# MoE 0's experts: each tile's first weights brought by a transfer instead of a VectorE copy, and VectorE's order within a tile changed

## What is computed

```
logits = tokens @ router_w.T;  probs = softmax(logits)
rw, re = top_k(probs, 2);      rw = rw / rw.sum()
out = tokens
for e in range(8):
    h = gelu(tokens @ w1[e] + b1[e])         # w1[e] is 256 x 256 in layer 0, 256 x 1024 in layer 1
    y = h @ w2[e] + b2[e]
    out = out + combine[:, e:e+1] * y        # combine holds rw for the two chosen experts, else 0
```

## Time and profile before

| | us |
|---|---|
| median of 3 runs | 2578.47 |
| lowest and highest | 2574.83, 2580.76 |
| the profiled execution | 2575.45 |
| its span in the profile | 2573.7 |

### The profile page before, as it was taken

How to read it: one execution, slowest core, us unless ns; L and a number is a source line. 1 busy time by engine, 2 the same in 40 slices (tenths; PEclk the granted TensorE clock), 3 DMA queues, 4 the chain that set the end, 5 groups by cost and what they waited for, 6 DMA issues and landing times. The chain is left out here.

```text
span 2573.7 us, 84276 instructions
## 1 busy us (share of the span) xinstructions
PE 2011.3 (78%) x28546; PEld 1511.0 (59%) x28547; DVE 2174.8 (85%) x3745; ACT 1674.1 (65%) x2530; POOL 789.6 (31%) x587
## 2 busy tenths in 40 slices
PE   4739999999999999999966158703598309999994
PEld 3316666666666666666645146501286209999993
DVE  4989999999999999999977747678798757777775
ACT  5439999999999999999965335403255535555551
POOL 2652212113222232422221734405111642222220
PEclk8869999999999999999987579955799559999996
DMA  2002323323323223223222434330000561111115
GB/s 78 0 19 77 89 69 87 87 70 87 83 74 87 77 79 89 72 83 89 70 79 81 146 107 116 109 139 3 0 0 26 171 217 49 51 48 47 49 46 202
DMA packets 284540, 202.95 MB, mean 79 GB/s; under 512 B 153632, under 2 KB 260208, under 8 KB 284208
## 3 DMA queue, kind: packets, MB, share of 16 engines
q1 hardware_dynamic: 271216, 164.16, 22.4%
q0 software_dynamic: 12960, 35.73, 3.7%
q10 hardware_dynamic: 288, 2.10, 0.2%
HBM read 69.05 MB, written 108.60 MB: 69 GB/s over the span
## 5 line engine op out<-in xcount | busy, mean ns | idle before, releaser
L583 DVE TENSOR_TENSOR plow<-prob 128x1024 f16<-128x1024 f32 (+1 forms) x1024 | 1127.2, 1172 | 3.7 <-ACT prob L494 3.7
L494 ACT ACTIVATE prob<-scores 128x1024 f32<-128x1024 f32 x1024 | 999.9, 1025 | 88.5 <-PE scores L626 58.4
L646 PEld LDWEIGHTS outp<-vs,prob 128*128 128x128 bf16 x7680 | 515.1, 98 | 280.2 <-issue 220.8
L646 PE MATMUL outp<-vs,prob 128*128 (+1 forms) x7680 | 603.6, 193 | 24.9 <-DVE plow L583 12.2
L626 PE MATMUL scores<-qT,kT 128*128 (+1 forms) x2048 | 610.7, 380 | 7.5 <-DMA kT<-shift_rows 2.7
L648 PE MATMUL outp<-vs,plow 128*128 (+1 forms) x7680 | 601.2, 193 | 0.0
L648 PEld LDWEIGHTS outp<-vs,plow 128*128 128x128 f16 x7680 | 502.8, 97 | 57.5
L439 POOL TENSOR_TENSOR osum<-osb 128x128 f32<-128x128 f32 x64 | 250.4, 3912 | 811.5 <-DVE rec L588 811.5
L1495 POOL DMA_INDIRECT expert_rows<-m1eyo,m1edest x71 | 107.6, 1516 | 315.4 <-DVE m1eyo L1467 285.4
L1366 PE MATMUL m1eph<-m1exT,m1ew1c 128*128 128x128 f16 x3408 | 203.0, 220 | 0.4 <-ACT m1exT L1403 0.4
L1366 PEld LDWEIGHTS m1eph<-m1exT,m1ew1c 128*128 128x128 f16 x3408 | 194.1, 98 | 1.1 <-ACT m1exT L1403 0.6
(11 more groups left out here) (375 smaller groups left out, 3325.9 us busy)
## 6 DMA issues: line engine op xcount, KB each, us to landing
sorted_rows<-zero SPq DMA_DIRECT2D x128, 522.0 KB, 4.7
m1dstg<-in_L_ffn_W_dram SPq DMA_DIRECT2D x32, 512.0 KB
staged<-qk SPq DMA_DIRECT2D x73, 128.0 KB, 2.4
m0exr<-sorted_rows SPq DMA_DIRECT2D x71, 130.5 KB
m1exr<-sorted_rows SPq DMA_DIRECT2D x71, 130.5 KB, 2.1
m0cgot<-expert_rows SPq DMA_DIRECT2D x8, 1024.0 KB, 5.6
m1cgot<-expert_rows SPq DMA_DIRECT2D x8, 1024.0 KB, 7.9
tok<-in_x_dram SPq DMA_DIRECT2D x4, 1024.0 KB, 9.5
```

Of the source, the lines that this page charges most:

```text
L494: act.activation(prob[g % PBUF][:, :], scores[g % 2][:, :], ACT.Exp, scale=1.0 / (QK_SCALE * QK_SCALE)).then_inc(prob_ready, 1)
L583: dve.tensor_tensor(l[:, 0:n], p[:, 0:n], high(p)[:, 0:n], ALU.subtract).then_inc(low_ready, 1)
L646: pe.matmul(to, high(prob[g % PBUF])[:, cols], v, start=(g == 0 and i == 0 and j == 0), stop=False, skip_group_check=True)
```

## The change

In MoE 0 (`narrow`, F // 128 < 4) a DMA started by SP, `fetch`, brings each tile's first weights from the weights in SBUF to one of four places `w1c`, three tiles ahead, right behind the tile's row load. It waits on `h_ready` for the place to be free, loads the expert's number into a register of SP, and moves 2 KB in each of 128 partitions. TensorE's `first` waits for the transfer's semaphore `w1_in`. VectorE's copy, its wait on `h_ready` and its increment of `w1_ready` are gone from `aim` in MoE 0, and `aim(i+2)` stands at the end of VectorE's step instead of its head. `aim` loads the expert into one of four registers, and `rows_out`, in both MoEs, uses the register that `aim` loaded two tiles before instead of loading its own. MoE 1 keeps its copy and its order.

```diff
+    narrow = NF < 4
+    NX = NY = NR if narrow else 2
-        w1c = [sb(f"w1c{u}", [P, 2, KB, F], F16) for u in range(2)]
+        NW = NX
+        w1c = [sb(f"w1c{u}", [P, 2, KB, F], F16) for u in range(NW)]
@@ SP
+            def fetch(i, u):
+
+                if not isinstance(i, int) or i >= NW:
+                    sp.wait_ge(h_ready, (i - NW + 1) * NQ)
+                    sp.sem_inc(fetching, 1)
+                e = expert_of(sp, w_reg, i)
+                sp.dma_start(w1c[u % NW][:, :, :, :], w1[:, ds(e, 1)].squeeze(1)).then_inc(w1_in[u % NW], 16)
+
             def step(i, u, it, left):
                 if left > NX - 2:
                     load(i + NX - 1, u + NX - 1)
+                    if narrow:
+                        fetch(i + NX - 1, u + NX - 1)
 
             for i in range(NX - 1):
                 load(i, i)
+                if narrow:
+                    fetch(i, i)
@@ TensorE
-            def first(i, u):
+            def first(i, u, it):
                 pe.wait_ge(xt_ready, i + 3)
-                pe.wait_ge(w1_ready, i + 1)
+                if narrow:
+                    pe.wait_ge(w1_in[u % NW], uses(it, u, NW) * 16 + 16)
+                else:
+                    pe.wait_ge(w1_ready, i + 1)
@@ VectorE
-            reg = dve.alloc_register(name + "dve_expert")
-            y_reg = dve.alloc_register(name + "dve_y_expert")
+            regs = [dve.alloc_register(name + f"dve_expert{u}") for u in range(4)]
 
             def aim(i, u, it):
-                e = expert_of(dve, reg, i)
-                if not isinstance(i, int) or i >= 2:
-                    dve.wait_ge(h_ready, i * NQ - NQ)
-                dve.tensor_copy(w1c[u % 2][:, :, :, :], w1[:, ds(e, 1)].squeeze(1)).then_inc(w1_ready, 1)
+                e = expert_of(dve, regs[u % 4], i)
+                if not narrow:
+                    if not isinstance(i, int) or i >= 2:
+                        dve.wait_ge(h_ready, i * NQ - NQ)
+                    dve.tensor_copy(w1c[u % 2][:, :, :, :], w1[:, ds(e, 1)].squeeze(1)).then_inc(w1_ready, 1)
                 dve.wait_ge(x_in[u % NX], uses(it, u, NX) * 16 + 16)
@@ rows_out
-                e = expert_of(dve, y_reg, i)
+                e = the_expert(dve, regs[u % 4])
@@ VectorE's step
-                if left > 1:
+                if left > 1 and not narrow:
                     aim(i + 2, u + 2, it)
                 if left > 0:
                     halve(i + 1, u + 1)
                 rows_out(i, u, it)
+                if left > 1 and narrow:
+                    aim(i + 2, u + 2, it)
```

More of the change, by code:

```diff
@@ L1268, in experts @@
     NQ = NF // 2
-    NX = NY = NR if NF < 4 else 2
+    narrow = NF < 4
+    NX = NY = NR if narrow else 2
     U = 2 * NR
@@ L1295, in experts @@
         w1_ready = sem("w1_ready")
+        w1_in = [sem(f"w1_in{u}") for u in range(NW)]
+        fetching = sem("fetching")
         h_ready = sem("h_ready")
@@ L1334, in load @@
                 sp.dma_start(xr[u % NX][:, :], sorted_dram[ds(row, P), :]).then_inc(x_in[u % NX], 16)
+            w_reg = sp.alloc_register(name + "sp_expert")
+            def fetch(i, u):
[4 more added lines that the diff above has]
+                sp.dma_start(w1c[u % NW][:, :, :, :], w1[:, ds(e, 1)].squeeze(1)).then_inc(w1_in[u % NW], 16)
             def step(i, u, it, left):
@@ L1366, in first @@
                                 last = pe.matmul(ph[(u * NQ + j) % 4][:, h * ET:(h + 1) * ET],
-                                                 w1c[u % 2][:, w, k, f * P:(f + 1) * P], xT[u % 2][:, x, :],
+                                                 w1c[u % NW][:, w, k, f * P:(f + 1) * P], xT[u % 2][:, x, :],
                                                  start=(k6 == 0), stop=(k6 == 3 * KB - 1))
@@ L1389, in step @@
                 if left > 0:
-                    first(i + 1, u + 1)
+                    first(i + 1, u + 1, it)
                 second(i, u)
@@ L1395, in _ @@
             turn(1, 1, 0)
-            first(0, 0)
+            first(0, 0, 0)
             pipelined(pe, step)
```

## The result

| | us |
|---|---|
| after, median of 4 runs (lowest, highest) | 2602.22 (2599.34, 2605.92) |
| before, on the same chip, median of 4 | 2577.06 (2574.83, 2580.76) |
| ratio, 95% interval | 1.0094 [1.0075, 1.0113] |
| the profiled execution of after (span) | 2604.65 (2602.9) |

The account below looks back on a forecast made before the run. The prediction took VectorE and its register loads in MoE 0 to set the pace; looped tiles 7.8, written-out tiles 2.9 and start 0.7 gave +11.4 us, hence 2590 us, range 2575 to 2608.

Parts of the forecast that it names:

- The ring: In MoE 0, `dest`, gelu, cast, low half and next `b1c` follow in series: 2.37 us a tile looped, 2.28 written out.
- `dest` to cast: In MoE 0's tile: `dest` 0.21, handover to ScalarE 0.17, two gelus 0.63, their end to VectorE's cast 0.10 us.
- rival 2: ScalarE's two further waits cost nothing and the loop's branch vanishes in the wait: 2.05 to 2.12 a tile, 2569 us; chance 0.08.
- Low half to `b1c`: On VectorE, waits and issue of L1467, then register load, wait and issue of `b1c`: 0.86 us looped, 0.77 written out.
- rival 1: VectorE's register load runs ahead of L1467's execution: 2.22 us a looped tile, about 2579 us, no change; chance 0.17.
- Cast to low half: On VectorE in MoE 0, from the start of the cast to the low half: 0.33 us a tile.
- The loop's sum: MoE 0's looped tiles average 2.40 us against 2.26 before, 7.8 us over 56 tiles.
- the branch: The loop's branch back every eighth tile: its own idle hidden in VectorE's wait for the gelu, 0.03 us a tile staying.
- Written-out tiles: MoE 0's tiles outside the loop: 12 at the steady pace go from 2.04 to 2.28 us, 2.9 us together.
- Start: At the start of MoE 0, three fetches go out with the first rows: 0 to 2 us, taken as 0.7.
- The transfer at nothing: In MoE 0's loop, the 256 KB fetch a tile costs nothing: DMA total 1.65 to 2.08 us fits into 2.40.
- rival 3: SP's fetch issue takes 1.2 us instead of 0.95 and the branch costs SP too: step 2.5 to 2.6, 2596 us; chance 0.05.

Follow-up runs that it names:

- no fast cast: The changed kernel with MoE 0's cast and bias copy written as two-input operations with the same result; 2.67 us a looped tile.
- scatter later: The changed kernel with GpSimd starting a tile's MoE 0 scatter only once the cast of the tile two on is done; ratio 1.0077 to before.
- aim first: The changed kernel with `aim(i+2)` put back at the head of VectorE's step in MoE 0; 2585.92 us, ratio 1.0027 to before.

## Why the prediction was right in sign and low in size

- **What bounded the kernel before: right.** VectorE with its register loads. Taking one load away gave 0.39 a tile, more than its visible gap of 0.2: 0.31 of it ahead of L1467 (0.65 to 0.34), 0.08 behind it.
- **The ring: right.** The forecast had the ring at 2.3 to 2.7, and it is 2.60, the gelu released by `dest`, the cast by ScalarE, L1488 close behind the low half (0.34), no copy, as listed. No branch idle of its own either: VectorE's longest "issue" ahead of `b1c` is 0.9, and `dest` to cast is nowhere above 1.05 in the loop.
- **`dest` to cast: forecast 0.21 + 0.17 + 0.63 + 0.10 = 1.11, measured 0.97 written out, 0.98 looped.** The gelu follows `dest`'s end by 0.17 in half of the loop's positions (1596.90 - 1596.73), by 0.03 in the others, and the cast follows the gelu's end by 0.04 (1597.56 - 1597.52), not 0.10, since VectorE is already standing in the wait. This is the piece of rival 2 that is true: waits behind the blocking one cost little.
- **Low half to `b1c`: forecast 0.77 written out and 0.86 looped; measured 0.83 and 1.12.** This is the term that failed in the loop. I had split it into a register load and waits by the rows of before, where the copy and a wait on TensorE lay around the load, and took the loop's excess over written-out tiles (0.09) from there. Without the scatter it is 0.34 + 0.66 = 1.00, the prediction's upper bound (0.99, the load starts only with L1467); the scatter adds 0.12. So rival 1, the load hidden under L1467 and a ring of 2.22, is refuted: only where the load was moved away did `b1c` follow at 0.34.
- **Cast to low half: forecast 0.33, measured 0.39 in the loop.** GpSimd was named nowhere in the prediction. The change moves the cast from right behind `dest` to 0.9 behind it, into the scatter. Before, no cast was longer than 305 ns.
- **The loop's sum.** 2.40, plus 0.04 for `b1c` to `dest`, less 0.13 ahead of the cast, plus 0.06 for the cast, plus 0.26 behind the low half, less the 0.03 put on for the branch, is the 2.60 measured. 0.18 of it is the scatter. The kernel without it stands at 2.42, next to the forecast, but by errors that cancel: that agreement is luck.
- **Written-out tiles: forecast 0.24 each for 12, 2.9 us; measured 1.2 for five ahead of the loop and 2.1 for the last five.** Of the first ones only one has a held cast, and four take 2.21 or 2.22; the last ones run like the loop.
- **Start: forecast 0.7; measured 2.7 in tiles 1 to 4.** Not the transfers: from the first row load to the first `b1c` it is 4.85 us (1506.43 - 1501.58), about as before. The order costs it: tile 2's `b1c` now stands behind two low halves and `rows_out(0)`, at 1514.25 instead of 1510.59, which puts TensorE's time into the ring while its clock is still low. After from 1512, and the kernel without the scatter at the same step, from 1515 (length, PE, PEld, DVE, ACT, POOL, PEclk, DMA share, GB/s):

```profile
1512.00:1514.00 2.00, 1.92 (x13) 1.55 (x14) 1.03 (x3) 0.00 (x0) 0.00 (x0) 0.50 0.62 198
...
1515.00:1517.00 2.00, 1.88 (x26) 1.78 (x26) 1.44 (x5) 0.61 (x2) 0.00 (x0) 1.00 0.58 198
```

With the clock at 1.00 there, tiles 1 to 4 take 11.23 without the scatter and 11.68 with it (no fast cast); with the clock at 0.50 they take 13.23 (after) and 13.02 (scatter later). So some 1.5 to 2 us of the 13.23 are the low clock. Before had the low clock in these tiles too (10.55), but TensorE's time was not yet in VectorE's ring. The prediction priced the start by the transfers alone.
- **The transfer at nothing: right for after, by a narrow margin that I did not see.** The 1.57 us of DMA time a tile (57.2% of 195 us over 71) and the fit of the bytes were as forecast (1.65 to 2.08). SP's step was put at 2.05 from an issue distance of 0.95; in aim first it is 2.12 at best and 2.35 on the mean, rival 3's mechanism at a smaller size. It hides below a ring of 2.60 and shows as soon as the ring is shortened. And of the register's gain the sum booked only what lay in the ring; alone it was 26 us on one chip and 12 on another.

With the edits added in this order, the loop's 0.34 a tile (forecast 0.14) are: -0.39 registers, +0.48 transfer through SP, +0.25 ring and scatter. The first two of these the prediction never set side by side, and their sum of +0.09 is what aim first measures. In another order the parts come out otherwise: after's own tile is set by the ring of 2.60, below which SP's 2.35 costs nothing. The last part, and the first, also compare chips that may differ.

## What to carry to other kernels

Price each edit of a change against the kernel that has only the others: here one edit won 26 us (12 on another chip) and two hid it. A copy that is moved to a DMA costs its issuing queue a wait, a register load and a DMA, about 1.2 us a tile (2.12 for the pair against 0.95 for a load alone), which counts as soon as that queue feeds another stage. When a step is moved behind a wait, list what the other engines do at its new time, not only what it waits for.

## What the hardware showed beyond the forecast

- A cast of 0.29 us took up to 0.54 when it began 0.51 to 0.73 us into GpSimd's indirect DMA, and then always ended at 1.05; from 0.74 on it wasn't held. The two-input form of the same size (0.42) never changed (424 to 427 ns).
- In the loop, a register load that stands between two VectorE instructions costs 0.32 without GpSimd (0.66 against 0.34) and 0.44 with it (0.78), and nothing inside a long wait (0.34).
- On SP a row load plus a fetch, with a register load each, take about 2.35 us on the mean, whether the fetch moves 256 or 64 KB.
- The same kernel stood at 0.9901 and 0.9952 of before on two chips, with intervals that don't touch: a gain of half a per cent can depend on the chip.
